# The last layer-norm step of the attention stages, moved from DVE to POOL in a two-layer decoder kernel

## The chip, the core and the metric

One core of a Trainium2 chip runs the whole program. The metric is device time of one execution in microseconds, the median of three runs. TensorE is called PE, VectorE DVE, ScalarE ACT, GpSimd POOL and SyncE SP; each has its own instruction queue and works through it in order, and the queues meet only at semaphores.

## The reference, cut to what matters

Input is x of 32 x 64 tokens of 128 features, and a context of the same shape. Six stages follow each other, and each ends in the same way, with a layer norm that has no gain and no bias:

```
def _layernorm(x, axis=-1, eps=1e-05):
    m = jnp.mean(x, axis=axis, keepdims=True)
    v = jnp.var(x, axis=axis, keepdims=True)
    return (x - m) / jnp.sqrt(v + eps)
...
x = _layernorm(x + rotary self attention(x))           # stage 0, 16 heads of 8
x = _layernorm(x + cross attention(x, ctx))            # stage 1, layer norm on each head of q and k
x = _layernorm(x + FP4 gated feed-forward(x))          # stage 2
x = _layernorm(x + linear attention block(x))          # stage 3
x = _layernorm(x + causal cross attention(ctx, x))     # stage 4
x = _layernorm(x + mixture of 8 experts, top 2(x))     # stage 5
```

Everything is float32 up to the masks.

## The kernel before, in words

The 2048 tokens are cut into four chunks of 512 tokens, a chunk into 4 tiles of 128 tokens on the 128 partitions. Two streams (`first`, `second`, in the text A and B) each carry one chunk through stages 0 to 4; then each takes a second chunk (`h.turn` 0 and 1, in the text the two passes). After that the mixture of experts runs over all tokens at once.

Every engine's program is written as generators, one for stream A, one for stream B and one for the experts, which give way at each `yield`. `weave` runs them through one queue by a fixed list of counts, `ORDER["pe"]`, `ORDER["act"]`, `ORDER["dve"]`, `ORDER["pool"]`. So the order of instructions of each engine is fixed when the program is built, and an instruction that waits holds up all behind it, those of the other stream too.

At the end of a tile t of stage `sub` these steps follow each other:

- `sum_norm` on DVE: L1377 adds the residual to the projection into `r` (two buffers, by t % 2), L1380 takes the statistics, L1383 reduces them to mean and variance `mv`. Before L1377 DVE waits until the norm of the tile two before has been written (L1376), since it reuses the buffer.
- `rstd` on POOL: L1954 adds eps to the variance, L1957 raises it to the power -1/2 into `rs`. The two are separate steps of the generator, so that a step of the other stream can stand between them.
- `norm_x` on DVE: L1389 (to L1390) writes (r - mean) * rs, a 128x128 tile, into `x`, or for stage 4 into `pay`, and counts up the semaphore `x_new`.

`x_new` has these readers: PE's `turn_x` (L602, transposes at L603) waits for the four tiles one by one and starts the next stage's projections; DVE's `quantize_x` (L1527) waits for tiles 1 and 3 of stage 1 before it starts the FP4 steps (L1345 to L1370); POOL's `residual` (L1973, L1974) waits for all four; and `sum_norm` itself. Stages 0, 1 and 4 are the attention stages: on DVE they interleave, tile by tile, the row maximum of the scores (L1408), its subtraction (L1413), the reciprocal (L1423) and division (L1426), the sum and statistics of an earlier tile, and the norm of the tile before that. Stage 0 has the head norms of stage 1 as its tail (L1464 to L1511, `heads_norm`) and stage 1 the first half of the quantization.

POOL also spreads the keys (`spread_keys`, L1985, two 128x512 operations each time), adds the biases (L1974), makes the power for the linear block (L1963, L1967) and issues the indirect DMAs of the routing (L1998) and of the experts (L2007).

Of the kernel before, what the change touches and what calls it, by code (L numbers as in the profile page):

```python
# [25 lines left out]
ALU = mybir.AluOpType  # L26
# [5 lines left out]
P = 128  # L32
# [54 lines left out]

HEADS_NORM, ROTATED = 17, 4
KEEP_BUSY = 26
MATS_FIRST = 6  # L90


# [134 lines left out]
def decoder(nc, x_in, ctx_in, mats_in, cols_in, fp4_gu_in, fp4_d_in, fc1_in, fc1b_in, fc2_in, bp_in, bo_in,  # L227
            router_in, wg_in, wu_in, eb_in, wo_in, bout_in, tables_in, cmask_in, identb_in, ranks_in,
            rows_io, shares_io, base_io, out):
    with ExitStack() as ctx:  # L230
# [277 lines left out]
        def _(sp):  # L508
# [4 lines left out]
            def load_context(c, k):  # L513
                sp.dma_start(streams[k].cin[:, :, :], tiles(ctx_in, c, k)).then_inc(streams[k].c_here.sem, 16)

            def load_x(c, k):
                sp.dma_start(streams[k].xin[:, :, :], tiles(x_in, c, k)).then_inc(streams[k].x_here.sem, 16)
# [44 lines left out]
            load_x(0, 0)  # L562
            sp.dma_start(mats[:, 0:MATS_FIRST, :], mats_in[:, 0:MATS_FIRST, :]).then_inc(mats_here, 16)
            load_x(0, 1)
# [4 lines left out]
            for k in range(STREAMS):  # L569
                load_context(0, k)  # L570
            sp.dma_start(mats[:, MATS_FIRST:, :], mats_in[:, MATS_FIRST:, :]).then_inc(more_mats_here, 16)
            sp.dma_start(bp[:, :], bp_in.partition_broadcast(P)).then_inc(biases_here, 16)
# [24 lines left out]
        def _(pe):  # L597
# [372 lines left out]
            def blocks_of_experts():  # L970
# [31 lines left out]
                def keep_busy():  # L1002

                    pe.wait_ge(xbT_here, BLOCKS)
                    for _ in range(KEEP_BUSY):
                        pe.matmul(ps[:, 0, :].rearrange("p (h k) -> p h k", k=S), identb[:, :],
# [327 lines left out]
        def _(dve):  # L1334
# [47 lines left out]
                dve.wait_ge(*h.stat.at(n))  # L1382
                dve.bn_aggr(h.mv[:, t % 2, :], h.st[:, t % 2, :]).then_inc(h.mean_here.sem, 1)  # L1383

            def norm_x(h, sub, t, src=None):
                yield
                dve.wait_ge(*h.rstd_here.at(sub * TILES + t + 1))
                dst = h.pay[:, t, 0:P] if sub == 4 else h.x[:, t, :]
                dve.tensor_scalar(dst, h.r[:, t % 2, :] if src is None else src,  # L1389
                                  h.mv[:, t % 2, 0:1], h.rs[:, t % 2:t % 2 + 1], ALU.subtract, ALU.mult).then_inc(h.x_new.sem, 1)  # L1390

            def attention_tiles(h, n, sub, res, tail={}):
                base = n * TILES
                for u in range(TILES + 5):
# [6 lines left out]
                    if 0 <= u - 5:  # L1401
                        yield from norm_x(h, sub, u - 5)
# [130 lines left out]
            def ffn(h):  # L1533
                yield
                yield from quantize_x(h, 1)
                for u in range(TILES + 3):
                    if 0 <= u - 2 < TILES:
                        yield
                        dve.wait_ge(*h.projected.at(2 * TILES + u - 1))
                        yield from sum_norm(h, 2, u - 2, h.ps[:, 3, 0:P], h.x[:, u - 2, :])  # L1540
                    if 0 <= u - 3:
                        yield from norm_x(h, 2, u - 3)
                    if u < TILES:
                        t = u
                        yield
                        dve.wait_ge(*h.silu_here.at(t + 1))
                        if t >= 2:
                            dve.wait_ge(*h.hq_turned.at(t - 1))
                        dve.tensor_tensor(h.hq[:, t % 2, 0:FFN], h.sg[:, t % 2, :], h.ps[:, 1, 0:FFN], ALU.mult).then_inc(h.hidden.sem, 1)
                        yield  # L1550
                        dve.wait_ge(*h.hidden.at(t + 1))
                        if t:
                            dve.wait_ge(*h.hq_here.at(t))
                        else:
                            dve.wait_ge(*h.ffn_x.at(2))
                        h3 = h.hq[:, t % 2, 0:FFN].rearrange("p (b k) -> p b k", k=BLOCK)
                        ins = yield from quantize(h, h3, h3, FFN // BLOCK, h.fq, 8 * (t + 2))
                        ins.then_inc(h.hq_here.sem, 1)
# [47 lines left out]
            def linear_block(h):  # L1606
# [62 lines left out]
                for u in range(TILES + 1):  # L1669
                    if u < TILES:  # L1670
                        if u:
                            yield
                        yield from sum_norm(h, 3, u, h.ps[:, 1, tile(u)], h.x[:, u, :])
                    if u >= 1:
                        yield from norm_x(h, 3, u - 1)
# [273 lines left out]
        def _(pool):  # L1949
            def rstd(h, sub, t):  # L1950
                n = sub * TILES + t + 1
                yield
                pool.wait_ge(*h.mean_here.at(n))
                pool.tensor_tensor(h.rs[:, t % 2:t % 2 + 1], h.mv[:, t % 2, 1:2], eps[:, 0:1], ALU.add).then_inc(h.eps_added.sem, 1)  # L1954
                yield
                pool.wait_ge(*h.eps_added.at(n))
                pool.tensor_tensor(h.rs[:, t % 2:t % 2 + 1], h.rs[:, t % 2:t % 2 + 1], minus_half[:, 0:1],  # L1957
                                   ALU.pow).then_inc(h.rstd_here.sem, 1)

            def block_rstd(h, n):  # L1960
                yield
                pool.wait_ge(*h.block_dve.at(BLOCK_DVE[f"n_mean {n + 1}"]))
                pool.tensor_tensor(h.nrs[:, :].rearrange("p (t o) -> p t o", o=1), h.nmv[:, :, 1:2],  # L1963
                                   eps[:, :].rearrange("p (t o) -> p t o", o=1), ALU.add).then_inc(h.block_pool.sem, 1)
                yield
                pool.wait_ge(*h.block_pool.at(BLOCK_POOL[f"n_eps {n + 1}"]))
                pool.tensor_tensor(h.nrs[:, :], h.nrs[:, :], minus_half[:, :], ALU.pow).then_inc(h.block_pool.sem, 1)  # L1967
# [52 lines left out]
            def norms(h, sub):  # L2020
                for t in range(TILES):
                    yield from rstd(h, sub, t)
# [127 lines left out]
```

## Time and profile before

| | |
|---|---|
| runs | 738.24 us median of 3 (737.21 to 739.14) |
| span of the profiled execution | 763.1 us, mean granted TensorE clock 0.837 |
| DVE busy | 531.9 us, 70% |
| PE busy | 568.6 us, 75% |
| ACT busy | 327.7 us, 43% |
| POOL busy | 200.5 us, 26% |
| L1389 on DVE | 80 instructions, 48 of them in the attention stages |

The profile has the span of its execution and no separate time of it: the span is 24.9 us above the median of the runs shown. How to read it: the busy shares are averages over stages with different limits. The chain of work that ended last is followed back from the last instruction, at each step to what released it or to the instruction before it on its engine, so only a piece that stands in the chain can shorten the run by its own length.

### The profile page before, as it was taken

The numbers are of one execution on the slowest core, as the hardware profiler recorded it, in microseconds if no ns is written. First come the engines' busy times: TensorE is split into PE (matmuls) and PEld (weight loads), VectorE is DVE, ScalarE is ACT, GpSimd is POOL, SyncE is SP. The second block draws the span as 40 slices with busy tenths as digits, with TensorE's granted clock in tenths as the row PEclk, the third lists the DMA queues.
The fourth block names the chain that finished last, engine by engine and source line by source line (L and its number), as shares of the span: only waits on it lengthen the run. The fifth ranks groups of instructions, "written<-read, shape, count | busy, mean of one in ns | idle before, by whom it ended". The sixth has DMA issues, their size and how long they took to land.

```text
span 763.1 us, 13948 instructions
## 1 busy us (share of the span) xinstructions
PE 568.6 (75%) x4890; PEld 393.2 (52%) x4890; DVE 531.9 (70%) x1520; ACT 327.7 (43%) x642; POOL 200.5 (26%) x312
## 2 busy tenths in 40 slices
PE   5787668756788688775975784667886987679984
PEld 2466546534455347442764463444542675567861
DVE  9667677888667667673686778996855767455633
ACT  2653445312474465142634451126744632344632
POOL 2204201201203502046043011121024034454543
PEclk9897669667699989687888797777997885599998
DMA  9993000000000000011000000000000001132215
GB/s 276 326 298 98 28 1 2 1 0 0 2 1 0 1 1 3 1 33 54 2 6 0 1 2 1 0 2 0 2 0 1 2 1 40 58 96 68 78 54 155
DMA packets 45556, 32.34 MB, mean 42 GB/s; under 512 B 4281, under 2 KB 43457, under 8 KB 45361
## 3 DMA queue, kind: packets, MB, share of 16 engines
q1 hardware_dynamic: 41104, 25.49, 12.1%
q0 software_dynamic: 2272, 4.92, 1.9%
q10 hardware_dynamic: 2112, 1.05, 0.5%
q8 instruction: 40, 0.66, 0.4%
q14 instruction: 28, 0.22, 0.1%
HBM read 13.83 MB, written 17.62 MB: 41 GB/s over the span
## 4 chain that ended last, share of the span: by engine, by line
PE 43%; DVE 32%; ACT 11%; issue 7%; POOL 4%; another core or an unknown queue 2%; DMA 1%; DVEq 0%; ACTq 0%; POOLq 0%
PE ps L643 5%; PE ps L984 5%; PE ps L624 5%; PE ps L687 5%; DVE s_row_max L1408 2%; PE ps L998 2%; ACT s_probs L1135 2%; DVE s_probs L1413 2%; DVE s_r L1377 2%; PE ps L655 2%; PE ps L906 1%; PE ps L911 1%; DVE s_st L1380 1%; DVE s_work L1367 1%
## 5 line engine op out<-in xcount | busy, mean ns | idle before, releaser
L1954 POOL TENSOR_TENSOR s_rs<-s_mv,eps 128x1 f32<-128x1 f32 x80 | 17.1, 215 | 349.3 <-DVE s_mv L1383 349.2
L1408 DVE TENSOR_REDUCE s_row_max<-ps 128x16 f32<-128x1024 f32 x48 | 58.7, 1222 | 62.3 <-PE ps L643 47.2
L1115 ACT ACTIVATE s_pT<-ps 128x512 f32<-128x512 f32 x96 | 55.5, 594 | 56.6 <-PE ps L624 44.2
L624 PE MATMUL ps<-tabs,s_probs 128*128 128x128 f32 x384 | 64.2, 302 | 19.8 <-ACT s_probs L1135 12.2
L643 PE MATMUL ps<-s_k,s_q 64*64 64x256 f32 x768 | 64.8, 451 | 13.5 <-ACT s_q L1085 9.9
L624 PEld LDWEIGHTS ps<-tabs,s_probs 128*128 128x128 f32 x384 | 45.8, 152 | 40.7 <-issue 19.9
L1135 ACT ACTIVATE s_probs<-s_probs 128x1024 f32<-128x1024 f32 x48 | 50.6, 1055 | 24.0 <-DVE s_probs L1413 23.7
L1413 DVE TENSOR_TENSOR s_probs<-ps,s_row_max 128x1024 f32<-128x1024 f32 x48 | 58.7, 1222 | 1.3
L687 PE MATMUL ps<-s_v,s_pT 128*64 128x18 f32 x1536 | 54.9, 216 | 3.5 <-issue 1.4
L687 PEld LDWEIGHTS ps<-s_v,s_pT 128*64 128x64 f32 x1536 | 51.0, 143 | 12.0 <-issue 11.0
L984 PE MATMUL ps<-s_pT,s_k 128*128 128x128 f32 x312 | 48.4, 304 | 3.8 <-issue 1.6
L1985 POOL TENSOR_SCALAR s_k<-s_kT,tabs 128x512 f32<-128x512 f32 x24 | 38.1, 1596 | 45.9 <-DVE s_kT L1442 28.8
L2007 POOL DMA_INDIRECT shares_io<-s_qT,y_row x39 | 38.0, 975 | 42.5 <-ACT s_qT L1284 38.1
L643 PEld LDWEIGHTS ps<-s_k,s_q 64*64 64x64 f32 x768 | 32.2, 156 | 31.1 <-issue 13.5
L984 PEld LDWEIGHTS ps<-s_pT,s_k 128*128 128x128 f32 x312 | 42.9, 213 | 8.4 <-issue 6.5
L1957 POOL TENSOR_TENSOR s_rs<-s_rs,minus_half 128x1 f32<-128x1 f32 x80 | 44.9, 565 | 5.2
L1879 DVE SCALAR_TENSOR_TENSOR s_pT<-ps,s_k,s_pT 128x128 f32<-128x128 f32 x78 | 23.7, 345 | 28.2 <-ACT s_pT L1274 19.8
L1274 ACT ACTIVATE s_pT<-ps,s_k 128x128 f32<-128x128 f32 x78 | 24.5, 367 | 37.7 <-PE ps L984 22.8
L1998 POOL DMA_INDIRECT rows_io<-s_work,s_slot x32 | 31.3, 977 | 16.7 <-issue 9.2
L1065 ACT ACTIVATE s_xT<-ps 128x512 f32<-128x512 f32 x20 | 11.9, 594 | 49.3 <-PE ps L603 24.4
L809 PE MATMUL ps<-gu_w,s_xT 128*128 128x352 f32 x64 | 30.8, 625 | 1.1 <-ACT s_xT L1065 1.1
L998 PE MATMUL ps<-wo,s_pT 128*128 x156 | 27.1, 298 | 5.6 <-ACT s_qT L1284 5.6
(288 smaller groups left out, 1247.8 us busy)
## 6 DMA issues: line engine op xcount, KB each, us to landing
rows_io<-zero_rows SPq DMA_DIRECT2D x9, 1152.0 KB, 11.9
s_probs<-rows_io SPq DMA_DIRECT2D x39, 72.0 KB
s_xin<-in_x SPq DMA_DIRECT2D x4, 256.0 KB, 4.1
s_cin<-in_ctx SPq DMA_DIRECT2D x4, 256.0 KB, 4.1
wgu<-in_wg SPq DMA_DIRECT2D x1, 1024.0 KB
wgu<-in_wu SPq DMA_DIRECT2D x1, 1024.0 KB
wo<-in_wo SPq DMA_DIRECT2D x1, 1024.0 KB
out_x<-s_work SPq DMA_DIRECT2D x4, 256.0 KB, 2.3
```

The costliest lines, as they stand in the source:

```text
L624: ins = pe.transpose(h.ps[:, 2, tile(j)], h.probs[:, t % 2, 8 * part + 2 * j:8 * part + 2 * j + 2, :] .rearrange("p h k -> p (h k)"), ident)
L643: ins = pe.matmul(h.ps[S * b:S * b + S, half, 256 * side:256 * side + 256], h.q4[rows, side, S * sq:S * sq + S], h.k4[rows, sq, :, :].rear ...
L687: ins = pe.matmul(h.ps[S * b:S * b + S, 3, 18 * j:18 * j + 18], h.pT[:, t % 2, j, S * b:S * b + S], h.v2[:, 2 * t + b, 2 * j:2 * j + 2, :] ...
L984: ins = pe.matmul(ps[:, 1 + b % 2, tile(m)], wb[:, b % WDEPTH, tile(m)], xbT[:, b % 2, :], start=True, stop=True)
L998: ins = pe.matmul(ps[:, 3, 0:P], bhid[:, b % 2, tile(m)], wo[:, bass.ds(e, 1), m, :].rearrange("p e d -> p (e d)"), start=m == 0, stop=m == 1)
L1115: act.activation(h.pT[:, t % 2, 4 * part:4 * part + 4, :].rearrange("p j q -> p (j q)"), h.ps[:, 2, :], ACT.Copy).then_inc(h.pT_here.sem, 1)
L1135: act.activation(h.probs[:, u % 2, :, :], h.probs[:, u % 2, :, :], ACT.Exp).then_inc(h.exped.sem, 1)
L1408: dve.tensor_reduce(h.row_max[:, t % 2, :], s3, AX, ALU.max).then_inc(h.max_here.sem, 1)
L1413: dve.tensor_tensor(h.probs[:, t % 2, :, :], s3, h.row_max[:, t % 2, :].rearrange("p (h o) -> p h o", o=1).to_broadcast([P, H, S]), ALU.su ...
L1957: pool.tensor_tensor(h.rs[:, t % 2:t % 2 + 1], h.rs[:, t % 2:t % 2 + 1], minus_half[:, 0:1], ALU.pow).then_inc(h.rstd_here.sem, 1)
L1985: ins = pool.tensor_scalar(h.k4[:, :, m, :], seqs(h.kT[:, :]), tab("member")[:, m:m + 1], None, ALU.mult)
L2007: pool.indirect_dma_start(shares_io, bass.IndirectOffsetOnAxis(ap=y_row[:, g % 3, k:k + 1], axis=0), yb[:, b % YDEPTH, :], None).then_inc( ...
```

## The change

In stages 0, 1 and 4 DVE's `norm_x` issues nothing (it still gives way once, so that the order list fits as before), and POOL issues the same operation on the same operands right behind its power, with a wait for the power's semaphore. Stages 2 and 3 keep the norm on DVE. There are 2 streams x 2 passes x 3 stages x 4 tiles = 48 such operations. No DMA is added or moved, and no buffer.

```diff
 KEEP_BUSY = 26
+POOL_NORMS = (0, 1, 4)
 MATS_FIRST = 6
...
-            def norm_x(h, sub, t, src=None):
-                yield
+            def norm_x(h, sub, t):
+                yield
+                if sub in POOL_NORMS:
+                    return
                 dve.wait_ge(*h.rstd_here.at(sub * TILES + t + 1))
-                dst = h.pay[:, t, 0:P] if sub == 4 else h.x[:, t, :]
-                dve.tensor_scalar(dst, h.r[:, t % 2, :] if src is None else src,
-                                  h.mv[:, t % 2, 0:1], h.rs[:, t % 2:t % 2 + 1], ALU.subtract, ALU.mult).then_inc(h.x_new.sem, 1)
+                dve.tensor_scalar(h.x[:, t, :], h.r[:, t % 2, :], h.mv[:, t % 2, 0:1], h.rs[:, t % 2:t % 2 + 1], ALU.subtract, ALU.mult).then_inc(h.x_new.sem, 1)
...
                 pool.wait_ge(*h.eps_added.at(n))
                 pool.tensor_tensor(h.rs[:, t % 2:t % 2 + 1], h.rs[:, t % 2:t % 2 + 1], minus_half[:, 0:1],
                                    ALU.pow).then_inc(h.rstd_here.sem, 1)
+                if sub in POOL_NORMS:
+                    pool.wait_ge(*h.rstd_here.at(n))
+                    dst = h.pay[:, t, 0:P] if sub == 4 else h.x[:, t, :]
+                    pool.tensor_scalar(dst, h.r[:, t % 2, :], h.mv[:, t % 2, 0:1], h.rs[:, t % 2:t % 2 + 1],
+                                       ALU.subtract, ALU.mult).then_inc(h.x_new.sem, 1)
```

## Rows read from the trace of the kernel before

**Rows 1.** The page: busy time of each engine, and the chain by engine.

```profile
PE 568.6 (75%) x4890; PEld 393.2 (52%) x4890; DVE 531.9 (70%) x1520; ACT 327.7 (43%) x642; POOL 200.5 (26%) x312
...
PE 43%; DVE 32%; ACT 11%; issue 7%; POOL 4%; another core or an unknown queue 2%; DMA 1%; DVEq 0%; ACTq 0%; POOLq 0%
```

**Rows 2.** Source view of L1389: min/median/max ns, waits before it.

```profile
L1389 DVE TENSOR_SCALAR s_x<-s_r,s_mv,s_rs x64: 309/337/927, 57.5 to 584.1; 128x128 f32<-128x128 f32 x64
L1389 DVE TENSOR_SCALAR s_work<-s_r,s_mv,s_rs x16: 312/316/347, 297.9 to 632.2; 128x128 f32<-128x128 f32 x16
...
  POOL s_rs L1957: 5.7, 12
```

**Rows 3.** Instruction groups of POOL by form: busy us, mean ns, idle before.

```profile
L1957 POOL TENSOR_TENSOR s_rs<-s_rs,minus_half 128x1 f32<-128x1 f32 x80 | 44.9, 565 | 5.2
L1985 POOL TENSOR_SCALAR s_k<-s_kT,tabs 128x512 f32<-128x512 f32 x24 | 38.1, 1596 | 45.9 <-DVE s_kT L1442 28.8 <-PE ps L906 9.2 <-ACT s_kT L1105 7.8
...
L1954 POOL TENSOR_TENSOR s_rs<-s_mv,eps 128x1 f32<-128x1 f32 x80 | 17.1, 215 | 349.3 <-DVE s_mv L1383 349.2
...
L1974 POOL TENSOR_TENSOR s_resid<-s_x,bp 128x512 f32<-128x512 f32 x4 | 5.1, 1267 | 0.0
...
L2014 POOL TENSOR_SCALAR s_heads<-s_heads 128x4 f32<-128x4 f32 x4 | 0.9, 231 | 0.0
```

**Rows 4.** The chain by time, 60 to 70 us: start, length, what.

```profile
63.51 0.35 DVE s_x L1389
...
69.31 0.70 DVE s_probs L1511
```

**Rows 5.** The chain by time, 458 to 463 us.

```profile
461.24 0.03 issue
461.27 0.35 DVE s_x L1389
```

**Rows 6.** The chain by time, 620 to 633 us.

```profile
625.46 1.05 PE ps L603 x4
...
631.44 0.24 DVE s_work L1389
...
632.24 0.26 DVE s_work L1389
```

**Rows 7.** Timeline of POOL, 620 to 633.5 us: start, length, idle before.

```profile
622.27 1.07 POOL L1957 TENSOR_TENSOR s_rs<-s_rs,minus_half 128x1 f32<-128x1 f32 x2
623.52 0.25 POOL L1954 TENSOR_TENSOR s_rs<-s_mv,eps 128x1 f32<-128x1 f32 x1 [0.18 <-DVE s_mv L1383]
623.84 0.60 POOL L1957 TENSOR_TENSOR s_rs<-s_rs,minus_half 128x1 f32<-128x1 f32 x1
```

**Rows 8.** Timeline of POOL, 299 to 306 us.

```profile
300.07 1.07 POOL L1957 TENSOR_TENSOR s_rs<-s_rs,minus_half 128x1 f32<-128x1 f32 x2
...
304.16 0.60 POOL L1957 TENSOR_TENSOR s_rs<-s_rs,minus_half 128x1 f32<-128x1 f32 x1
```

**Rows 9.** Timeline of DVE, 79 to 83 us; the tile's power ended at 80.11.

```profile
81.94 0.34 DVE L1389 TENSOR_SCALAR s_x<-s_r,s_mv,s_rs 128x128 f32<-128x128 f32 x1
```

**Rows 10.** Timeline of DVE where 128x512 operations of POOL run beside it.

```profile
84.28 0.44 DVE L1495 TENSOR_SCALAR s_work<-s_work 128x64 f32<-128x64 f32 x1
84.76 0.63 DVE L1499 TENSOR_SCALAR s_work<-s_work 128x64 int32<-128x64 int32 x1
85.42 0.20 DVE L1502 TENSOR_SCALAR s_work<-s_work 128x64 int32<-128x64 int32 x1
...
75.33 1.35 DVE L1499 TENSOR_SCALAR s_work<-s_work 128x64 int32<-128x64 int32 x1
```

**Rows 11.** Timeline of POOL in the same stretches.

```profile
83.11 3.11 POOL L1985 TENSOR_SCALAR s_k<-s_kT,tabs 128x512 f32<-128x512 f32 x2 [2.99 <-ACT s_kT L1105]
...
75.36 1.28 POOL L1974 TENSOR_TENSOR s_resid<-s_x,bp 128x512 f32<-128x512 f32 x1
```

**Rows 12.** Timeline of DVE, 476.5 to 479.2 us, where POOL's power ended at 477.84.

```profile
478.25 0.34 DVE L1358 TENSOR_SCALAR s_work<-s_work 128x352 int32<-128x352 int32 x1
```

## The prediction

> **What bounds the kernel now.** I read the page first. DVE is busy 70% and POOL 26% of the span, and the chain that ended last lies 32% on DVE, 43% on PE and 4% on POOL [rows 1]. No engine is full; two streams in fixed queues wait for each other, so what counts is which pieces stand in the chain. DVE's share of it makes relief of DVE worth looking at, and POOL's 349.2 us of waiting for means [rows 3] shows that POOL has room. But the room is there because POOL waits for the very tile whose norm it is now to make: its new work comes when its data comes, not in the empty time.
>
> Second, the moved instruction. On DVE it takes 337 ns into `x` and 316 ns into `pay` (medians), and DVE stood idle before it only 12 times in 80, for 5.7 us in all [rows 2]. So in most cases the power was ready long before DVE came to the norm, and mean, power and norm do not form one chain. They do at the last tile of a stage, where the next stage hangs on it: 461.27 follows the power that ended 0.03 us before [rows 5].
>
> Third, the chain by time. In the attention stages 19 of its pieces are L1389, 4.95 us together, from 63.51 to 632.24 [rows 4, 6]. Fifteen are norms that DVE makes on its way to something else, 3.7 us, the first 0.35 at 63.51 and the last 0.24 at 631.44. Four belong to the last tile of a stage (151.92, 461.27, 478.07, 632.24), and what comes next needs their result.
>
> The durations are from one execution with a span of 763.1 us, 24.9 above the median of 738.24. My terms are differences of a few us made of DVE and POOL instructions; 3% of them is nothing, so I put the sum on the median.
>
> **Removed from DVE.** 48 instructions x 0.33 us = 16 us of DVE's 531.9. Only what stands in the chain pays: 3.7 us for the fifteen, and 15 x 0.02 = 0.3 us of the gaps around them (the "issue" piece of 0.03 in [rows 5] is the largest of them). Term: -4.0. The other 29 norms gave way to waits that stay: they run beside PE or ACT work that sets the next step. If that cover is gone, up to 29 x 0.33 = 9.6 us would be open, but then some other piece would have to leave the chain first.
>
> **Added on POOL.** Its price is not in the trace. The nearest rows are POOL's own tensor_scalar: 231 ns at 4 columns and 1596 ns at 512, so 2.69 ns a column, and 0.23 + 124 x 0.00269 = 0.56 us at 128 [rows 3]. That operation has one arithmetic step and one scalar column, the new one two of each. Below, the addition of 512 columns at 1267 ns gives 2.05 ns a column, hence 0.46 us. Above, with the slope doubled for the second step, 0.90 us. I take 0.60, near the row of the same instruction.
>
> The GPSIMD Engine Reference of the Trainium skill (section 4.1, engine selection) says that an elementwise operation with one tensor input runs at about line rate there. By it the new operation would be no slower than DVE's, some 0.35 us, an estimate from that page, and the sum would come out about 2 us lower. The row of 1596 ns for 512 columns speaks against it.
>
> POOL has no work that this displaces in bulk: 48 x 0.60 = 29 us, and its wait for the power is a gap of about 0.07 us like the one between its own two steps. What matters is who stands behind it and who waits for it.
>
> **Last tiles on the chain.** The new norm starts 0.07 after the power instead of 0.03, takes 0.60 instead of 0.35, and hands over to another engine. That is +0.3 us each, four times: +1.2. The waiters are DVE's L1527, with the whole quantization behind it in DVE's queue, and PE's L603, with both streams' matmuls behind it.
>
> **Two places where POOL queues.** At 622.27 two powers run back to back, one of each stream, and the last tile's eps and power follow at 623.52 and 623.84 [rows 7]. With a norm behind each power I get: B's norm 622.90 to 623.50, A's power to 624.12, A's norm to 624.80, eps, power to 625.70, norm to 626.37. DVE had the tile done at 624.83. PE begins the four transposes at 625.46 in the chain [rows 6] and reaches the fourth about 625.97: +0.4. At 300.07 the same pattern stands and the last power starts at 304.16 [rows 8]; it moves to 304.51, the norm ends 305.75 instead of 305.14: +0.6. Term: +1.0.
>
> **Earlier tiles.** Two last tiles of stream B were written by DVE 2.2 and 2.6 us after their power had ended, the first at 81.94 to 82.28 [rows 9]. POOL writes them sooner, and PE's wait of 0.11 us before each goes: -0.2. The buffer wait at L1376 is met everywhere, since DVE used to make the norm before it in the same queue.
>
> **DVE held by POOL.** At 84.76 an operation of 64 columns that needs 0.20 us takes 0.63 while POOL's L1985 has begun just before; at 75.33 it takes 1.35 beside L1974 [rows 10, 11]. Operations with a PSUM input show nothing of the kind. So DVE operations on SBUF alone are held up to 0.43 us by a tensor_scalar and over 1.1 by an addition. I set the places where the new operation would start (power's end + 0.08) beside DVE's timeline: in 14 of 48 such a DVE operation starts within 0.4 us, the first at 69.31 [rows 4], the last at 478.25 [rows 12]. They are head norms and FP4 steps. The bounds of the hold are 0 and 0.43; I take 0.2, since the new operation reads a quarter of the columns, and half of it in the chain: 14 x 0.2 x 0.5 = +1.4.
>
> **The sum.** -4.0 + 1.2 + 1.0 - 0.2 + 1.4 = -0.6 us, 737.6. What the measurement can tell from no change is about 0.3%, 2.2 us.
>
> **Rivals.**
>
> *The gain stays (faster).* If the new operation is at its low bound, 0.46, the last tiles cost 4 x 0.16 = 0.6 and the queues 0.3; if holds fall off the chain they cost nothing. -4.0 + 0.6 + 0.3 - 0.2 = -3.3, 734.9. For it: the chain counts only fifteen pieces, and half of the holds are guesswork. Against it: POOL's measured slope.
>
> *POOL is late at the end of a stage (slower).* One mechanism: mean, eps, power, norm at the last tile all in POOL's queue. At 0.90 us four tiles cost 0.6 each, 2.4; at 622 three norms in a row add 1.3 and at 300 1.2; three more last tiles that are now just off the chain join it, at 0.5 each, 1.5. With the holds at 1.4: -4.0 + 2.4 + 2.5 + 1.5 - 0.2 + 1.4 = +3.6, 741.8. It decides from about 0.8 us an operation. For it: two arithmetic steps and two scalars. Against it: POOL's instructions of one column differ by 0.35 us between add and power only.
>
> *DVE and POOL exclude each other (slower).* Each of the 14 DVE operations waits for the whole of POOL's, 0.6, and as DVE carries these stretches 60% of it shows: 5.0. -4.0 + 1.2 + 1.0 - 0.2 + 5.0 = +3.0, 741.2. For it the hold at 75.33; against it 84.76, where DVE went on after 0.43 us of an operation of 1.57. SBUF — State Buffer of the Trainium skill (section "SBUF: two separate sides") says that the pair of ports is an exclusive lock, held for the whole instruction. By that rule the full hold is right; the trace agrees for the addition and not for the tensor_scalar.
>
> That the change does not do what it says I leave out: the order lists stay in step.
>
> **Chances and range.** Forecast (within 2.2 us, own range 736.0 to 740.4) 0.46; gain stays 0.28; POOL late 0.17; exclusion 0.09. Hence faster 0.28, same 0.46, slower 0.26. The range 733.9 to 741.8 takes in the first rival with a us for the sizes of its terms, and the slower ones up to their computed times.
>
> **What would show it.** In the changed profile L1389 has 32 instructions and POOL 48 tensor_scalars of 128 columns, mean near 0.60. DVE busy falls by about 16 us, less the holds, and POOL's rises by 29. PE's wait at L603 and DVE's at L1345 name POOL's norm, 0.3 to 0.7 us each at last tiles. Head norm and FP4 operations show maxima of 0.4 to 0.6 where they had 0.2 to 0.5. I am wrong if the operation takes under 0.4 or over 0.8, if DVE's groups grow by more than 5 us, or if a wait names POOL in the middle of a stage.

## The result, and where the profile after differs

| | before | after |
|---|---|---|
| median of 20 runs each | 737.80 us (733.15 to 746.16) | 743.07 us (739.14 to 747.69) |
| ratio, 95% interval | | 1.0084 [1.0060, 1.0107] |
| profiled execution: time, span | span 763.1 us alone | 745.92 us, 744.0 us |
| DVE busy, instructions | 531.9 us, 1520 | 518.7 us, 1472 |
| POOL busy, instructions | 200.5 us, 312 | 240.1 us, 360 |

The change costs 5.3 us by the medians. The forecast was 737.6, "same"; the result is slower by more than its interval and lies outside the range of 733.9 to 741.8.

**Time and clock.** The TensorE clock that was granted, averaged over the span, differs from one execution of a kernel to the next: 0.827 to 0.865 over 105 executions of the kernel before. All 271 executions of this study, with a level of their own for each kernel, lie along a line that falls by 2.95 us (95%: 2.70 to 3.20) for each 0.01 of clock, with 1.6 us left over. Since the differences sought are of 1 to 5 us, the tables below give the ratio as measured and beside it the difference "at equal clock" from that fit. The changed kernel had 0.8476 on the mean, the kernel before 0.8507: +5.1 us in the means is +4.2 (±0.8) at equal clock and 0.9 of clock. Whether the change itself lowers the clock is not settled, and if it does, the equal-clock numbers leave that part out. The ratios leave out seven executions that ran over 1.5% above the fastest of their kernel, while the fit takes them in; without them experiment 5 is -0.5 ± 1.0, experiment 16 -1.2 ± 1.0, and no other difference moves by more than 0.4.

The page of the kernel after, busy time, the clock in 40 slices, and the chain by engine:

```profile
PE 563.2 (76%) x4890; PEld 388.6 (52%) x4890; DVE 518.7 (70%) x1472; ACT 327.4 (44%) x642; POOL 240.1 (32%) x360
...
PEclk9999659778689969868996597886999696699997
...
PE 42%; DVE 28%; ACT 11%; issue 7%; POOL 7%; DMA 2%; DVEq 0%; SPq 0%; POOLq 0%; ACTq 0%
```

Against [rows 1] DVE left the chain as hoped (32% to 28%), and POOL came in (4% to 7%). The slices of 5 and 6 are near the lower of the clock's two levels (1.2 of 2.4 GHz), the 9s near the upper one. What TensorE did ahead of those slices was not followed here; one such fall is under experiment 8.

The moved operation in the source view of its new line (min/median/max ns, then who waited for it):

```profile
L1963 POOL TENSOR_SCALAR s_x<-s_r,s_mv,s_rs x32: 792/797/1109, 57.0 to 471.9; 128x128 f32<-128x128 f32 x32
L1963 POOL TENSOR_SCALAR s_work<-s_r,s_mv,s_rs x16: 791/795/799, 299.5 to 627.3; 128x128 f32<-128x128 f32 x16
...
  PEld ps L604: 6.6, 5
  DVE s_qmax L1346: 5.3, 5
  PE ps L604: 4.8, 4
```

On DVE the same operation had medians of 337 and 316 ns [rows 2]; on POOL it takes 797 and 795. The groups by form of POOL after, which answer to [rows 3]:

```profile
L1958 POOL TENSOR_TENSOR s_rs<-s_rs,minus_half 128x1 f32<-128x1 f32 x80 | 45.1, 564 | 5.2
L1991 POOL TENSOR_SCALAR s_k<-s_kT,tabs 128x512 f32<-128x512 f32 x24 | 38.1, 1595 | 39.1 <-DVE s_kT L1443 26.9 <-PE ps L907 9.2 <-ACT s_kT L1106 2.9
L1963 POOL TENSOR_SCALAR s_x<-s_r,s_mv,s_rs 128x128 f32<-128x128 f32 x32 | 26.9, 840 | 3.4
...
L1955 POOL TENSOR_TENSOR s_rs<-s_mv,eps 128x1 f32<-128x1 f32 x80 | 17.1, 215 | 306.0 <-DVE s_mv L1384 305.9
...
L1963 POOL TENSOR_SCALAR s_work<-s_r,s_mv,s_rs 128x128 f32<-128x128 f32 x16 | 12.7, 795 | 1.7
```

26.9 + 12.7 = 39.6 us is the whole growth of POOL. Most of it came out of POOL's wait for means: 338.1 us in a second execution of the kernel before (experiment 1; the 349.2 of [rows 3] are of the execution that was 27 us longer), 305.9 now; the rest goes with a span that is 7.9 us longer. POOL had the room in bulk. What it lacked is shown by the end of the first pass of stage 1. DVE's timeline of the kernel before in that second execution (span 736.1; the executions differ in where a stage falls by some us):

```profile
448.99 0.18 DVE L1383 BATCH_NORM_AGGREGATE s_mv<-s_st 128x2 f32<-128x6 f32 x1
...
450.12 0.35 DVE L1389 TENSOR_SCALAR s_x<-s_r,s_mv,s_rs 128x128 f32<-128x128 f32 x1 [0.51 <-POOL s_rs L1957]
...
450.58 0.41 DVE L1345 TENSOR_REDUCE s_qmax<-s_x 128x16 f32<-128x256 f32 x1
```

The same place after, on DVE:

```profile
453.56 0.18 DVE L1384 BATCH_NORM_AGGREGATE s_mv<-s_st 128x2 f32<-128x6 f32 x1
...
455.65 0.42 DVE L1346 TENSOR_REDUCE s_qmax<-s_x 128x16 f32<-128x256 f32 x1 [1.39 <-POOL s_x L1963]
```

and on POOL:

```profile
453.82 0.19 POOL L1955 TENSOR_TENSOR s_rs<-s_mv,eps 128x1 f32<-128x1 f32 x1 [3.51 <-DVE s_mv L1384]
454.09 0.55 POOL L1958 TENSOR_TENSOR s_rs<-s_rs,minus_half 128x1 f32<-128x1 f32 x1
454.74 0.80 POOL L1963 TENSOR_SCALAR s_x<-s_r,s_mv,s_rs 128x128 f32<-128x128 f32 x1
```

From the start of the mean to the start of the quantization (`s_qmax`) it was 1.59 us and is now 2.09: +0.5. DVE, which used to wait 0.51 for the power, waits 1.39 with nothing to do, since the norm it would have made is POOL's.

### The profile page after: what moved, and what is told of

It reads as the page before. It is cut to its first block, busy times and chain, and to the rows that moved or that the text cites. A ratio compares the mean times of both kernels' runs of the same rounds, so it can differ in the third digit from the quotient of the medians.

```text
span 744.0 us, 13948 instructions
## 1 busy us (share of the span) xinstructions
PE 563.2 (76%) x4890; PEld 388.6 (52%) x4890; DVE 518.7 (70%) x1472; ACT 327.4 (44%) x642; POOL 240.1 (32%) x360
## 3 DMA queue, kind: packets, MB, share of 16 engines
q1 hardware_dynamic: 41104, 25.49, 12.4%
## 4 chain that ended last, share of the span: by engine, by line
PE 42%; DVE 28%; ACT 11%; issue 7%; POOL 7%; DMA 2%; DVEq 0%; SPq 0%; POOLq 0%; ACTq 0%
PE ps L644 6%; PE ps L625 5%; PE ps L688 4%; PE ps L985 4%; DVE s_row_max L1409 2%; PE ps L999 2%; ACT s_probs L1136 2%; DVE s_probs L1414 2%; POOL s_rs L1958 2%; PE ps L810 2%; DVE s_r L1378 2%; PE ps L907 2%; PE ps L611 1%; PE ps L912 1%; DVE s_work L1368 1%
## 5 line engine op out<-in xcount | busy, mean ns | idle before, releaser
L1955 POOL TENSOR_TENSOR s_rs<-s_mv,eps 128x1 f32<-128x1 f32 x80 | 17.1, 215 | 306.0 <-DVE s_mv L1384 305.9
L1991 POOL TENSOR_SCALAR s_k<-s_kT,tabs 128x512 f32<-128x512 f32 x24 | 38.1, 1595 | 39.1 <-DVE s_kT L1443 26.9
L985 PE MATMUL ps<-s_pT,s_k 128*128 128x128 f32 x312 | 44.6, 288 | 3.8 <-issue 2.4
L985 PEld LDWEIGHTS ps<-s_pT,s_k 128*128 128x128 f32 x312 | 39.4, 198 | 7.4 <-issue 5.7
L656 PE MATMUL ps<-mats,s_headsT 128*128 128x128 f32 x96 | 22.5, 327 | 8.8 <-DVE s_heads L1427 6.7
```

Of the source, the lines that this page charges most:

```text
L985: ins = pe.matmul(ps[:, 1 + b % 2, tile(m)], wb[:, b % WDEPTH, tile(m)], xbT[:, b % 2, :], start=True, stop=True)
L1991: ins = pool.tensor_scalar(h.k4[:, :, m, :], seqs(h.kT[:, :]), tab("member")[:, m:m + 1], None, ALU.mult)
```

## The experiments

Three theories stood against each other. **Late:** the change costs where a stage's last tile waits for POOL, by the slower operation (the expectations' 'last tile') and by POOL's queue ('queue'; the two together are 'place'). **Beside** ('hold'): POOL's new operations hold DVE up everywhere, as its longer ones do in [rows 10, 11]. **Every norm:** each tile's way became longer, and it shows in the middle of stages too. And the question that the sum left: where is the relief of 4.0 us?

| run | norms on POOL | ratio [95%] | at equal clock, us |
|---|---|---|---|
| after | all 48 | 1.0084 [1.0060, 1.0107] | +4.2 ± 0.8 |
| e2_first_three | 36, without last tiles | 1.0046 [1.0018, 1.0073] | +1.4 ± 1.0 |
| e3_last_only | 12 last tiles | 1.0106 [1.0072, 1.0140] | +5.3 ± 1.4 |
| e4_beside | none; 48 spare ones beside | 1.0086 [1.0056, 1.0116] | +3.4 ± 1.3 |
| e5_chosen | 25 early in POOL's free time | 0.9992 [0.9954, 1.0030] | −0.05 ± 1.0 |
| e6_stage0 | 16 | 1.0011 [0.9973, 1.0050] | −0.04 ± 1.0 |
| e7_stage1 | 16 | 1.0077 [1.0046, 1.0107] | +1.9 ± 1.0 |
| e8_stage4 | 16 | 1.0054 [1.0025, 1.0084] | +2.3 ± 1.0 |
| e10_twice | none; DVE makes 36 twice | 1.0122 [1.0079, 1.0166] | +5.3 ± 1.4 |
| e11_no_eps | none; no eps step | 1.0038 [1.0006, 1.0071] | +0.3 ± 1.0 |
| e12_stage4_first | 12 of stage 4 | 1.0035 [1.0002, 1.0068] | +2.0 ± 1.0 |
| e13_stage1_first | 12 of stage 1 | 0.9986 [0.9958, 1.0015] | −0.04 ± 1.0 |
| e14_stage1_last | 4 of stage 1 | 1.0075 [1.0046, 1.0103] | +2.7 ± 1.4 |
| e15_stage4_last | 4 of stage 4 | 1.0048 [1.0016, 1.0080] | +1.2 ± 1.0 |
| e16_chosen_no_eps | 25, no eps step | 1.0021 [0.9994, 1.0049] | −1.5 ± 1.0 |

### 1. The kernel before, once more

No edit: the first profile of it had a span 25 us above its runs.

> The kernel before once more, for a second profile, since the first one has a span of 763.1 us against 744.0 of the changed kernel although the changed kernel's runs are slower by 0.84%. Every theory expects a span near 736 us (the median of 737.8 less the 2 us by which the changed kernel's span lies under its own time), with no single gap of 11 us near 350 us.

Measured: 738.07 us, span 736.1, clock 0.851. Its page:

```profile
PE 559.1 (76%) x4890; PEld 387.9 (53%) x4890; DVE 531.1 (72%) x1520; ACT 326.7 (44%) x642; POOL 199.9 (27%) x312
...
PEclk9997669888799989878996595786999696699998
```

The busy times are those of [rows 1] within 2%, PE's differing most; the extra 27 us of the first profile were mostly idle time of the engines, 11.3 us of it in one gap at 350.75, which this one does not have. The clock falls in nearly the same slices as in the page of after. All comparisons of traces from here on use this one.

### 2 and 3. All but the last tiles, and the last tiles alone

Both from the changed kernel, with the same condition in `norm_x` (which then makes the others on DVE, into `pay` in stage 4) and behind the power; 3 has `==` in place of `<` and, so that the tiles' counts stay in order, a wait ahead of POOL's norm.

```diff
-                if sub in POOL_NORMS:
+                if sub in POOL_NORMS and t < TILES - 1:
...
+                    pool.wait_ge(*h.x_new.at(n - 1))
```

> POOL norms tiles 0 to 2 of each attention stage, DVE the last tile, so 36 of 48 stay moved. Theory 'last tile' (the 0.80 us of POOL's norm and the handing over stand in the chain where the next stage begins, 12 times): all of the 6 us comes back and the relief of DVE shows, ratio to before 0.995 to 1.000. Rival 'hold' (DVE operations on SBUF are held while POOL norms): three quarters of the cost stay, ratio near 1.006. Rival 'queue' (a norm in POOL's queue makes the other stream's eps and power late): most of it stays too, since the norms of tiles 0 to 2 stand ahead of the last tile's power, ratio 1.003 to 1.006.

> POOL norms only the last tile of each attention stage, DVE tiles 0 to 2 (POOL also waits there for the norm of tile 2, which DVE has long written). 12 of 48 are moved. Theory 'last tile': all of the cost with none of the relief, ratio 1.008 to 1.011. Rival 'hold': a quarter of the cost, ratio near 1.002. Rival 'queue': little, ratio 1.000 to 1.004, since nothing stands ahead of the last power that did not before.

Measured: +1.4 ± 1.0 for the 36 early ones (as measured 1.0046, what 'queue' had said), +5.3 ± 1.4 for the 12 last ones (1.0106, what 'last tile' had said). Most of the cost sits at the last tiles, as "late" has it; the 36 others, three quarters of the relief of DVE, bring nothing back.

### 4. The operation beside, with nobody waiting for it

From the kernel before: POOL also makes an operation of the same form on data of its own, behind each of the 48 powers.

```diff
+                if sub in (0, 1, 4):
+                    pool.wait_ge(set_up, len(SET_UP) + len(spares))
+                    pool.wait_ge(*h.rstd_here.at(n))
+                    pool.tensor_scalar(spare[:, :], ident, tab("member")[:, 0:1], tab("member")[:, 1:2], ALU.subtract, ALU.mult).then_inc(set_up, 1)
+                    spares.append(n)
```

> The kernel before, with all norms on DVE, and POOL runs an operation of the same form, 128x128 with two scalar columns, on constants into a spare tile behind each of the 48 powers. Nobody waits for its result; it has POOL's time, its place in POOL's queue and its hold on the port, and neither relieves DVE nor delays a norm by itself. Theory 'last tile': only what the queue adds, ratio 1.000 to 1.003. Rival 'hold' and rival 'queue': the cost of the change plus the relief that is missing here, ratio 1.010 or more. DVE's busy time against the kernel before tells the two apart: it grows by some 6 us under 'hold' and not under 'queue'.

Measured: +3.4 ± 1.3, as measured 1.0086, which lies between what the expectation gave to 'last tile' (up to 1.003) and to the two others (1.010 or more). That fits "beside", and it also fits the queue: the spare operation stands ahead of the next eps and power just as the norm does. The trace tells the two apart. Its page:

```profile
PE 563.2 (76%) x4890; PEld 389.6 (53%) x4890; DVE 530.7 (72%) x1520; ACT 327.4 (44%) x642; POOL 243.8 (33%) x360
```

DVE was busy for 531.1 us in experiment 1, so hardly any DVE instruction became longer. And the last tiles of stream A in stage 4 are late although DVE makes their norm: from the end of the mean to the end of the norm it takes 2.33 and 3.10 us in the two passes, 1.34 and 1.38 in experiment 1. In the changed kernel itself only 6 DVE operations were held by a norm of POOL, 0.09 to 0.14 us each. One of them is the third row of DVE's timeline after:

```profile
77.63 0.23 DVE L1465 TENSOR_TENSOR s_work<-s_work 128x64 f32<-128x64 f32 x1
77.89 0.23 DVE L1468 SCALAR_TENSOR_TENSOR s_work<-s_work 128x64 f32<-128x64 f32 x1
78.15 0.36 DVE L1471 SCALAR_TENSOR_TENSOR s_work<-s_work 128x64 f32<-128x64 f32 x1
78.54 0.23 DVE L1465 TENSOR_TENSOR s_work<-s_work 128x64 f32<-128x64 f32 x1
```

beside this on POOL, which ran to 78.79:

```profile
77.95 0.84 POOL L1963 TENSOR_SCALAR s_x<-s_r,s_mv,s_rs 128x128 f32<-128x128 f32 x1
```

DVE's operation ends at 78.51, in the middle of POOL's, and the next takes its usual 0.23 us while POOL still runs. What each of the late tiles is worth of the 3.4 us was not measured.

### 5. Only where POOL has time and DVE needs it

25 tiles, chosen by the trace: POOL is idle behind their power, and DVE came to the norm late enough.

```diff
-POOL_NORMS = (0, 1, 4)
+POOL_NORMS = {
+    (0, 0, 0, 0), (0, 0, 0, 2), (0, 0, 1, 0), (0, 0, 1, 2), (0, 0, 4, 0),
...
-                if sub in POOL_NORMS:
+                if (streams.index(h), h.turn, sub, t) in POOL_NORMS:
```

> POOL norms only those 25 of the 48 tiles where in the trace of the kernel before two things hold: DVE came to the norm over 0.7 us after the power had ended, and POOL had nothing to do for 0.9 us behind the power. Theory 'place' (the cost lies at last tiles that the next stage waits for, and at norms that stand ahead of another tile's eps or power in POOL's queue; elsewhere a norm on POOL is free): nothing of the cost is left and the relief of DVE shows, 1 to 4 us faster than before, ratio 0.995 to 0.999. Rival 'every norm costs' (whatever POOL's operation does to DVE or to memory ports, it does each time): 25/48 of the cost, 2.2 us slower, ratio 1.003.

(As in experiment 3, POOL also waits for the norm of the tile before.)

Measured: −0.05 ± 1.0 us. Both expectations missed: 'place' had said 1 to 4 us faster, 'every norm costs' 2.2 slower. Eleven of the prediction's fifteen pieces of the chain are among the 25 tiles, 2.7 of their 3.7 us, so that by its rule 2.7 us should have come back. Nor did POOL eat them up: in the trace no instruction waited for one of POOL's 25 norms, and no last tile takes more than 0.12 us longer from its mean to its norm than in experiment 1. So twenty-five norms fewer on DVE are worth nothing that 12 executions can show. This is the experiment that breaks the sum. The page:

```profile
PE 561.5 (76%) x4890; PEld 389.2 (53%) x4890; DVE 526.0 (72%) x1495; ACT 327.2 (45%) x642; POOL 220.9 (30%) x337
...
PE 45%; DVE 29%; ACT 12%; issue 6%; POOL 4%; DMA 3%; SPq 0%; DVEq 0%; ACTq 0%; POOLq 0%
```

DVE was busy 5.1 us less than in experiment 1 and idle 3.2 us more. Its share of the chain fell from 32% to 29%, and PE's rose from 42% to 45%.

### 6 to 8. One stage at a time

```diff
-POOL_NORMS = (0, 1, 4)
+POOL_NORMS = (0,)
```

(and `(1,)`, `(4,)`; DVE's `norm_x` also gets its `pay` for stage 4 back, which matters in 6 and 7.)

> POOL norms stage 0 alone, 16 tiles. From the changed kernel's trace against the one before, the last tile's x comes 1.3 us later in one of four cases (pass 1, stream A) and 1.1 to 1.5 us sooner in three, where PE comes late anyway. Theory 'place': about 0, between 1 us faster and 1 us slower at equal clock. Rival 'every norm costs': a third of the cost, 1.4 us slower.

> POOL norms stage 1 alone, 16 tiles. Theory 'place': the last tile's x comes 0.5 us later after its mean in all four cases, and DVE, which waits for it with the quantization behind it, loses it each time: 2 us slower less the relief on tiles 0 to 2, so 0.5 to 2 us slower at equal clock. Rival 'every norm costs': 1.4 us slower. This one does not tell them apart by itself; it gives the share of the stage.

> POOL norms stage 4 alone, 16 tiles. Theory 'place': here the powers of both streams stand back to back on POOL, so that the last tile of stream A comes 1.2 and 2.0 us later after its mean and that of stream B 0.5 us later, with PE waiting each time: 2.5 to 4 us slower at equal clock, most of the whole. Rival 'every norm costs': 1.4 us slower.

Measured: −0.04, +1.9 and +2.3, each ± 1.0. Their sum is 4.2, the whole's is 4.2, so no interaction of the stages shows within some 1.7 us. That rests on the fit: as measured the three ratios are 1.0011, 1.0077 and 1.0054, more together than the 1.0084 of the whole, and the mean clock of experiment 7 was 0.843. Stage 4 alone costs a little less than the 2.5 to 4 us expected. Stage 0, where the chain of [rows 4] had its first norm, is neither gain nor loss with its 16.

Experiments 1 and 8 make a clean pair (spans 736.1 and 738.2, clocks 0.851 and 0.850; the same instants within 0.15 us up to stage 4 of the first pass). There the last tile of B comes 1.0 us later; 0.5 of it is left at 364 us and nothing at 449, so what is lost at this place was made up again. In the second pass the two are level until 612 us. The granted clock does not part them: in both it was 0.97 to 0.98 from 607 to 612 us, with TensorE busy for 4.0 to 4.1 of these 5 us, and 0.50, the lower level, from 612 to 620. POOL in the kernel before:

```profile
611.06 1.06 POOL L1957 TENSOR_TENSOR s_rs<-s_rs,minus_half 128x1 f32<-128x1 f32 x2
612.32 0.24 POOL L1954 TENSOR_TENSOR s_rs<-s_mv,eps 128x1 f32<-128x1 f32 x1 [0.19 <-DVE s_mv L1383]
612.63 0.60 POOL L1957 TENSOR_TENSOR s_rs<-s_rs,minus_half 128x1 f32<-128x1 f32 x1
```

and with stage 4's norms on POOL:

```profile
611.06 0.56 POOL L1959 TENSOR_TENSOR s_rs<-s_rs,minus_half 128x1 f32<-128x1 f32 x1
611.73 0.80 POOL L1964 TENSOR_SCALAR s_work<-s_r,s_mv,s_rs 128x128 f32<-128x128 f32 x1
612.49 0.56 POOL L1959 TENSOR_TENSOR s_rs<-s_rs,minus_half 128x1 f32<-128x1 f32 x1
613.15 0.80 POOL L1964 TENSOR_SCALAR s_work<-s_r,s_mv,s_rs 128x128 f32<-128x128 f32 x1
613.91 0.19 POOL L1956 TENSOR_TENSOR s_rs<-s_mv,eps 128x1 f32<-128x1 f32 x1
614.18 0.56 POOL L1959 TENSOR_TENSOR s_rs<-s_rs,minus_half 128x1 f32<-128x1 f32 x1
614.85 0.80 POOL L1964 TENSOR_SCALAR s_work<-s_r,s_mv,s_rs 128x128 f32<-128x128 f32 x1
```

The last tile of stream A in its second pass has its mean at the same time, 612.25, in both. Its eps starts 1.59 us later (613.91 for 612.32), because two norms and a power that were not there, or not so late, are ahead of it; its norm ends at 615.65, where DVE ended it at 613.62 in experiment 1 (613.27 and 0.35 in DVE's timeline): +2.0. TensorE, with the transposes of that tile (pass 2 of A, then of B), in experiment 8:

```profile
614.19 0.90 PE L604 MATMUL ps<-tabs,s_work 128*128 128x128 f32 x3
615.70 0.48 PE L604 MATMUL ps<-tabs,s_work 128*128 128x128 f32 x1 [0.60 <-POOL s_work L1964]
...
622.59 0.47 PE L604 MATMUL ps<-tabs,s_work 128*128 128x128 f32 x1 [2.27 <-POOL s_work L1964]
```

and in experiment 1:

```profile
614.26 1.12 PE L603 MATMUL ps<-tabs,s_work 128*128 128x128 f32 x4
...
621.41 0.47 PE L603 MATMUL ps<-tabs,s_work 128*128 128x128 f32 x1 [0.32 <-DVE s_work L1389]
```

Before, the four transposes of A ran in one go; now the fourth waits. The last one of B starts 1.18 us later: 0.7 because its mean came later, 0.5 for the norm itself. The run ends 2.1 later, but not by carrying these 1.2 to the end. TensorE's matmuls are 1.1 to 1.6 us later up to 648 us and only 0.06 at 650.46, behind a DMA of 4.30 us that stands in the chain; they are 0.9 later at 716.6 and 2.0 at 720.6, where the granted clock of the last 16 or 17 us was 0.85 in experiment 1 and 0.70 in 8. So this pair shows how the tiles come late; what that is worth only the executions tell (+2.3 ± 1.0).

### 9. Prices of the operation

The kernel before with operations on spare data behind its last store: three each of 128 columns with two steps and two scalars, 128 with one of each, 64 and 4 with two; then six of 128 beside bursts of DVE operations on 64 columns.

```diff
+            for width, first_scalar, second_scalar, op in ((128, a, b, ALU.mult), (128, a, None, None), (64, a, b, ALU.mult), (4, a, b, ALU.mult)):
...
+                        ins = pool.tensor_scalar(spare_p[:, at:at + width], ident[:, 0:width], first_scalar, second_scalar, ALU.subtract, op)
...
+            for _ in range(6):
+                pool.wait_ge(y_mean, CHUNKS + 1 + _)
+                pool.tensor_scalar(spare_p[:, at:at + P], ident, a, b, ALU.subtract, ALU.mult).then_inc(set_up, 1)
```

> The kernel before, and behind its end, when nothing else runs, POOL's operations by themselves (three each, one after the other): 128 columns with two steps and two scalar columns; 128 columns with one step; 64 and 4 columns with two steps. Then six of the first kind, each with a short operation of DVE and four DVE operations of 64 columns on SBUF started at the same time, three times with one input and three times with two. If the second step is what makes 0.80 us of my 0.56, the one-step operation takes 0.56 and the two-step one 0.80; if it is something in the kernel, the two-step one takes under 0.7 alone. The hold: if it is for the whole instruction, the first of DVE's four ends over 0.7 us after POOL's start; if it is for a part, 0.3 to 0.5.

Measured, POOL's groups by form from 734 us on (L2089 are the six beside DVE):

```profile
L2089 POOL TENSOR_SCALAR wgu<-tabs 128x128 f32<-128x128 f32 x6 | 5.4, 899 | 2.2 <-DVE mats L1952 2.2
L2083 POOL TENSOR_SCALAR wgu<-tabs 128x128 f32<-128x128 f32 x3 | 2.4, 794 | 4.0 <-DMA out_x<-s_work 3.8
L2081 POOL TENSOR_SCALAR wgu<-tabs 128x128 f32<-128x128 f32 x3 | 1.8, 603 | 0.3
L2083 POOL TENSOR_SCALAR wgu<-tabs 128x64 f32<-128x64 f32 x3 | 1.7, 578 | 0.3
L2083 POOL TENSOR_SCALAR wgu<-tabs 128x4 f32<-128x4 f32 x3 | 1.2, 384 | 0.3
```

With two steps and two scalars: 384 ns at 4 columns, 578 at 64, 794 at 128, so about 0.37 us and 3.3 ns a column. With one step the same 128 columns take 603 ns; the second step with its scalar costs 0.19. Beside DVE's bursts POOL's operation grows to 0.90 on the mean, while DVE's own did not grow (all twelve of a kind lie within 15 ns): it is POOL that loses. The bursts ended 0.2 to 0.4 us after POOL's start, so a hold late in the operation was not tested here.

### 10. The same norms, twice on DVE

From the kernel before: DVE makes the 36 norms of the tiles that are not the last of a stage a second time, into spare memory, ahead of the real one.

```diff
+                if sub in (0, 1, 4) and t < TILES - 1:
+                    spares.append(0)
+                    dve.tensor_scalar(spare[:, len(spares) % 3, :], h.r[:, t % 2, :], h.mv[:, t % 2, 0:1], h.rs[:, t % 2:t % 2 + 1], ALU.subtract, ALU.mult)
```

> The kernel before, and DVE makes the norm of tiles 0 to 2 of the attention stages twice, the first time into a spare tile: 36 more DVE operations of 0.33 us at the very places from which the change took them away, 12 us in all. The prediction's step 'what stands in the chain pays' holds for work added as for work taken away: 3 to 5 us slower at equal clock. If DVE has slack at these places, as the unchanged time of the 25 chosen tiles suggests, 0 to 1 us.

Measured: +5.3 ± 1.4 us, for 36 x 0.33 = 12 us of added DVE work. So some 45% of an added norm shows (5.3 ± 1.4 of 12 us), and none of a removed one (experiment 5).

### 11 and 16. A shorter way through POOL, alone and with the chosen norms

Experiment 11 is the kernel before without its eps step: the power reads the variance itself, so eps is left out of the layer norms of stages 0 to 4. Experiment 16 is that edit in experiment 5.

```diff
-                pool.tensor_tensor(h.rs[:, t % 2:t % 2 + 1], h.mv[:, t % 2, 1:2], eps[:, 0:1], ALU.add).then_inc(h.eps_added.sem, 1)
                 yield
-                pool.wait_ge(*h.eps_added.at(n))
-                pool.tensor_tensor(h.rs[:, t % 2:t % 2 + 1], h.rs[:, t % 2:t % 2 + 1], minus_half[:, 0:1],
+                pool.tensor_tensor(h.rs[:, t % 2:t % 2 + 1], h.mv[:, t % 2, 1:2], minus_half[:, 0:1],
```

> The kernel before without the addition of eps (the output lacks 1e-5 in the variance): POOL's way from mean to power is 0.27 us shorter at all 80 tiles and nothing else changes. Theory 'the way through POOL at the last tiles is what costs': 2 to 4 us faster at equal clock, for some twelve to sixteen last tiles on the chain. If the way through POOL does not matter, 0 to 1 us.

> The 25 chosen tiles on POOL and no addition of eps at any tile (the output lacks 1e-5 in the variance). Each alone made nothing faster (0.0 and 0.4 us). Theory 'tied paths' (DVE's work and POOL's way are two of several paths of nearly the same length between the same waits, so shortening one shows nothing and lengthening one shows whole): together 1 to 3 us faster. If neither lies on a path that binds, or a third one (TensorE) is as long: 0 within 1 us again.

Measured: +0.3 ± 1.0 for the shorter way of POOL alone (where the expectation had 2 to 4 us faster if POOL's way at the last tiles is what costs: longer it costs, shorter it gains nothing), −0.05 ± 1.0 for DVE's relief alone, −1.5 ± 1.0 for both. As measured, without the clock (0.841 in 16, 0.8507 before), 16 is 1.0021 [0.9994, 1.0049]: the gain of both together rests on the fit, and is a hint. So does the 0.3: as measured 11 is 1.0038 [1.0006, 1.0071], slower with work taken away, at a clock of 0.845.

### 12 to 15. First and last tiles of stages 4 and 1

The conditions of experiments 2 and 3 with one stage in `POOL_NORMS`; for the first of them:

```diff
-POOL_NORMS = (0, 1, 4)
+POOL_NORMS = (4,)
...
+                if sub in POOL_NORMS and t < TILES - 1:
```

> POOL norms tiles 0 to 2 of stage 4, DVE the last tile and all other stages. Against stage 4 as a whole (2.4 us slower at equal clock) this leaves only POOL's queue: norms that stand ahead of the last tile's eps and power. Theory 'queue at stage 4': 1 to 2 us slower. If only the last tile's own norm cost: 0 or faster.

> POOL norms tiles 0 to 2 of stage 1 only (12 of 48), DVE its last tile. All of stage 1 on POOL costs 2.0 us at equal clock. If that is the last tile alone: 0 within 1 us, as in stage 0. If it is spread over the tiles: 1.5 us slower.

> POOL norms the last tile of stage 1 only (4 of 48). If the last tile is what costs in stage 1 (DVE's quantization waits for it, 0.5 us later in each of four cases): 2 us slower at equal clock, the whole of the stage's. If the cost is spread: 0.5 us slower.

> POOL norms the last tile of stage 4 only (4 of 48). With tiles 0 to 2 alone stage 4 costs 2.1 us of its 2.3, which the queue on POOL explains. If that is right, nothing stands ahead of the last tile here and it comes 0.5 us late: 0 to 1 us slower. If the last tile's own norm is the cost there as well: 2 us slower.

Measured: stage 1, first tiles −0.04 ± 1.0, last tiles +2.7 ± 1.4. Stage 4, first tiles +2.0 ± 1.0, last tiles +1.2 ± 1.0. In 14 DVE's quantization waits for POOL's norm as it did in the changed kernel:

```profile
460.88 0.42 DVE L1346 TENSOR_REDUCE s_qmax<-s_x 128x16 f32<-128x256 f32 x1 [1.51 <-POOL s_x L1965]
```

In stage 4 the first tiles cost as well, and it shows in the last one: from the end of A's mean of the last tile to the end of its norm it takes 1.34 and 1.38 us in the two passes of experiment 1, 1.99 and 2.86 with the first tiles' norms on POOL (12), 1.87 and 1.90 with the last's (15), 2.54 and 3.40 with all (8). That is the queue. Of stage 4's two numbers the first is at the top of its expectation (1 to 2 us) and the second just above its own (0 to 1); they add up to more than experiment 8's 2.3, within their intervals. Stage 1's two are as expected.

## Why the prediction was wrong, point by point

The mechanism is the rival "POOL is late at the end of a stage", whose computed 741.8 (+3.6) is close to the +4.2 at equal clock, and whose point of decision, 0.8 us an operation, is what the operation takes. It was given 17%. That the number comes so near is in part luck: the rival has −4.0 of relief and +1.4 of holds, both of which measured about 0, and +6.4 for late tiles and queues, where the runs showed 4.2 to 5.0.

- **"Only what stands in the chain pays", −4.0: the step that failed.** Measured: nothing. The chosen 25, with eleven of the fifteen pieces and 2.7 us of them, give −0.05 ± 1.0, stage 0 gives −0.04 ± 1.0, stage 1's first tiles −0.04 ± 1.0; these three don't rest on the fit, for as measured they are 0.9992, 1.0011 and 0.9986. The work was removed (in the changed kernel the page's busy time of DVE, which counts overlapping instructions once, fell by 12.4 us against experiment 1) and its share of the chain fell by 4 points, but the time did not. A chain is the way that ended last in one execution; where a second way is nearly as long, the removed piece gives place to it. In experiment 5 it gave place to PE, by the chain's shares; which waits took over, place by place, was not followed. Experiment 10 shows the other side of this: lengthening does cost. And 5, 11 and 16 hint that two ways are tied, DVE's and POOL's, of which one alone brings nothing; that is not shown. The text had said that the other norms "gave way to waits that stay"; it should have asked the same of the fifteen.
- **The operation, 0.60 us:** 0.795, alone and undisturbed. The row of 512 columns was one step with one scalar, as the text said; at 128 columns even that costs 603 ns, and the second step adds 0.19. The upper bound of 0.90 held it; the choice "near the row of the same instruction" was the error. The Trainium skill's GPSIMD Engine Reference (section 4.1, Engine selection) calls operations with one input roughly line-rate there, by which the prediction had put it at some 0.35 us, an estimate. That is off by more than a factor of two for this operation, and the measurement decides.
- **Last tiles, +0.3 each, +1.2:** the place was right, and so was the waiter (`s_qmax` L1346). It is +0.5 at the place shown above (1.59 and 2.09 us) and 0.5 to 0.6 from mean to norm at each of stage 1's four last tiles, 2.3 together; stage 1's alone cost 1.9 to 2.7.
- **Two places where POOL queues, +1.0:** right in mechanism and place (the pattern at 611.06 is that of [rows 7]), too small: about 2.0 us in stage 4 (experiment 12). Of the two places the one near 300 us, put at +0.6, was made up again by 449 us in experiment 8. The norm ahead was reckoned at 0.60, and the delay that B inherits from A (0.7 of its 1.18 us) was not reckoned.
- **Earlier tiles, −0.2:** the last tiles of B in stage 0 do come 1.2 and 1.5 us sooner after their mean in the changed kernel, but stage 0's number shows nothing of it.
- **DVE held by POOL, +1.4:** about 0. Six holds of at most 0.14 us, 0.8 us together, instead of 14 of 0.2.
- **DVE and POOL exclude each other (9%):** fell. At 77.95 POOL's 128-column operation began, DVE's L1471 ended 0.56 us later with POOL's still running, and the next took its usual time. The Trainium skill's SBUF — State Buffer (section "SBUF: two separate sides") has an exclusive lock, held for the whole instruction, also for a DVE operation with two SBUF inputs against a POOL operation that reads SBUF. L1471 is such an operation, and the trace does not agree: it was held for 0.13 us, not until 78.79.
- **The gain stays (28%):** fell with the first term.

With the terms as measured: 0 (relief) + 1.9 to 2.7 (stage 1's last tiles) + 2.3 (stage 4) + 0 (stage 0, holds) = 4.2 to 5.0, where +4.2 ± 0.8 was measured; each term is known to about 1 us. Of the signs named beforehand, three came up: an operation of 0.8 us and more (0.825 on the mean of the 48), a wait on POOL's norm, and DVE's busy down by 13 us of the 16 (531.9 to 518.7).

**Open.** Experiment 3's +5.3 ± 1.4 is more than 14 and 15 together (3.9), though within the intervals; in all three the norms wait for DVE's norm of the tile before, which was not tried apart. Experiment 4's 3.4 us are put down to the queue by exclusion and by the two late tiles. Experiments 3, 4, 7, 10, 14, 15 and 16 had mean clocks of 0.839 to 0.843, each 0.008 to 0.012 below that of the kernel before on the same chip and 2.7 to 4 standard errors away, so chance does not explain it: the kernel itself may move the clock. What an edit costs by way of the clock is then missing from its equal-clock number. Why the clock differs stays open. No version here is clearly faster than the kernel before: the chosen norms are even with it, and the −1.5 us of experiment 16 leave out eps.

## What to carry to other kernels

Before a step is given to an engine with room, ask what that engine is doing when the step's data comes: POOL waited 338 us for means, but the norm comes at the end of mean, eps and power, and there the added time is on the way of the one tile that a stage waits for. Price relief and burden apart: here 25 removed norms gave 0 while 36 added ones cost 5.3, so the share that an engine has in the chain bounds a gain and does not estimate it. Where two ways may be tied, which was only hinted at here, try shortening both before giving up either.

## What the runs showed of the hardware that was not expected

- The mean granted clock moves between executions of one kernel (0.827 to 0.865), and 0.01 of it goes with 2.95 us here, more than most of the effects. By its scatter of 0.008 the mean of six executions can be 0.3% off by that alone.
- POOL's operation with two steps costs about 0.37 us before the first column, and 2.4 to 2.5 times DVE's time at 128 columns (797 for 337 ns into `x`, 795 for 316 into `pay`).
- When the two meet, the loser is mostly POOL: its operation grew from 0.80 to 0.90 on the mean beside DVE's bursts, and to at most 1.11 in the changed kernel, while DVE's were held by it for 0.14 us at most. Beside POOL's addition of 512 columns (1.27 us) a DVE operation of 64 columns took 1.32 in the changed kernel too, as in [rows 10, 11].
